# Gated attention in a layered kernel: decay matrix by a low-rank bf16 product, a new order of the work, scores weighed in halves

## The reference

```python
x = concatenate([q, k, v], -1)
ig, fg = x @ Wi + bi, x @ Wf + bf             # one gate of each kind per row and head
log_f_cum = cumsum(log_sigmoid(fg))           # along the sequence
log_D = where(ltr, log_f_cum[s] - log_f_cum[t], -inf) + ig[t]
max_log_D = max(log_D, over t)
D = exp(log_D - max_log_D)
C = (qh @ kh^T / sqrt(16)) * D
normalizer = maximum(abs(sum(C, over t)), exp(-max_log_D))
h = (C / (normalizer + EPS)) @ vh             # then a layer norm inside each head, times ln_scale
```

## Time and profile before

| | us |
|---|---|
| median of 3 runs | 2189.09 (2188.45 to 2192.63) |
| the profiled execution's own time | 2187.51 |
| its span, first to last instruction | 2185.8 |
| `gated_attention` within it | 386.8 |

### The profile page before, as it was taken

One profiled execution on the slowest core, in us unless ns is written; L12 is line 12 of the kernel. 1 busy time (PEld: TensorE's weight loads), 2 busy tenths in 40 slices (PEclk: granted clock), 3 DMA queues, 4 the chain that ended last, 5 costly groups with the idle time before them and its releaser, 6 DMA issues. The chain is left out here.

```text
span 2185.8 us, 34619 instructions
## 1 busy us (share of the span) xinstructions
PE 1499.0 (69%) x11458; PEld 931.5 (43%) x11458; DVE 1441.3 (66%) x2920; ACT 1114.9 (51%) x1540; POOL 570.9 (26%) x910
## 2 busy tenths in 40 slices
PE   3349999999299848788753666548989855776111
PEld 3326555555277635454431233334555542444000
DVE  6648888886245337667764999824555556775796
ACT  4517777777112124333443788822434335777454
POOL 3412333333200032322231444110010001111663
PEclk9999999999599969888985567568999976788555
DMA  5643555553300022113101000011010120000111
GB/s 167 199 109 86 136 129 131 136 131 95 82 1 0 2 66 59 44 38 68 34 6 62 0 1 1 1 37 37 23 37 22 28 82 20 1 1 1 48 49 39
DMA packets 94834, 120.62 MB, mean 55 GB/s; under 512 B 26128, under 2 KB 78552, under 8 KB 90108
## 3 DMA queue, kind: packets, MB, share of 16 engines
q1 hardware_dynamic: 94716, 119.12, 21.2%
HBM read 79.30 MB, written 22.09 MB: 46 GB/s over the span
## 5 line engine op out<-in xcount | busy, mean ns | idle before, releaser
L610 DVE TENSOR_REDUCE ratt_nmax<-ratt_psS 128x2 f32<-128x512 f32 x512 | 318.2, 684 | 92.3 <-PE ratt_psS L502 92.0
L576 ACT ACTIVATE ratt_E<-ratt_psT 128x1024 f32<-128x1024 f32 x256 | 255.0, 1023 | 105.4 <-PE ratt_psT L524 105.4
L502 PE MATMUL ratt_psS<-ratt_K,ratt_Q 72*128 72x256 bf16 x1024 | 204.1, 283 | 38.8 <-DMA ratt_K<-context_parts 33.2
L524 PE MATMUL ratt_psT<-ratt_Q,ratt_K 75*128 75x256 bf16 x1024 | 195.7, 274 | 5.2 <-DMA ratt_Q<-ratt_rows 4.8
L537 PE MATMUL ratt_psO<-ratt_E,ratt_V 128*32 128x256 f32 x2048 | 137.9, 387 | 0.7 <-ACT ratt_E L576 0.7
L502 PEld LDWEIGHTS ratt_psS<-ratt_K,ratt_Q 72*128 72x128 bf16 x1024 | 79.8, 99 | 134.8 <-issue 64.1
L524 PEld LDWEIGHTS ratt_psT<-ratt_Q,ratt_K 75*128 75x128 bf16 x1024 | 99.4, 98 | 22.9 <-DMA ratt_Q<-ratt_rows 5.3
L1355 PE MATMUL gatt_psA<-gatt_DA,gatt_same 128*128 128x512 f32 x128 | 88.4, 780 | 25.3 <-DVE gatt_DB L1240 25.3
L1174 POOL TENSOR_TENSOR gatt_DA<-gatt_own,gatt_a 128x1024 f32<-128x1024 f32 x32 | 61.6, 1937 | 143.1 <-PE gatt_psA L1358 90.0
L3304 PE MATMUL final_psT<-final_identh,final_Z 128*128 128x128 f16 x64 | 8.2, 309 | 110.4 <-ACT final_Z L3338 110.4
L1238 DVE TENSOR_REDUCE gatt_mx<-gatt_psA 128x16 f32<-128x1024 f32 x32 | 39.0, 1220 | 64.0 <-PE gatt_psA L1358 63.4
(11 more groups left out here) (461 smaller groups left out, 4029.4 us busy)
## 6 DMA issues: line engine op xcount, KB each, us to landing
ratt_Q<-z_parts SPq DMA_DIRECT2D x32, 576.0 KB
ratt_K<-context_parts SPq DMA_DIRECT2D x96, 192.0 KB
gatt_V<-in_ctx_dram SPq DMA_DIRECT2D x16, 512.0 KB, 6.2
z_parts<-prep_ZS SPq DMA_DIRECT2D x48, 128.0 KB, 2.7
context_parts<-prep_CS SPq DMA_DIRECT2D x48, 128.0 KB, 2.3
head_sums<-ratt_O SPq DMA_DIRECT2D x64, 72.0 KB
all_X<-in_x_dram SPq DMA_DIRECT2D x8, 512.0 KB
prep_C<-in_ctx_dram SPq DMA_DIRECT2D x8, 512.0 KB
```

The costliest lines, as they stand in the source:

```text
L502: mm = nc.tensor.matmul(psS[:, RING[h], c * D:(c + 1) * D], Q9[0:R, buf, h, k % 2, c * P:(c + 1) * P], K9[0:R, buf, h, k % 2, :], start=Tr ...
L524: mm = nc.tensor.matmul(psT[:, p % 2, e, c, :], K9[0:RM, buf, h, u, c * P:(c + 1) * P], Q9[0:RM, buf, h, u, :], start=True, stop=True)
L576: nc.scalar.activation(E[:, 2 * b + p // 2, 2 * (p % 2):2 * (p % 2) + 2], psT[:, p % 2], ACT.Exp, scale=SCALE).then_inc(exped, 1)
L610: nc.vector.tensor_reduce(nmax[:, k % 2, h, :], psS[:, RING[h]].rearrange("p (c t) -> p c t", c=2), AX.X, ALU.max, negate=True).then_inc(m ...
```

## The change

Only `gated_attention`, two methods of `Heads` and one HBM tensor (`decay_rows`) change. `softmax_attention`, which also uses `Heads`, keeps its form.

- `spread_a`, `max_and_shift`, `DA`, `DB`, `same`, `own`, `mask` and the copy `CG` are gone; the gates read `CT` itself.
- After the running sums PE turns `a` (`turn_a`: 64 rows of 128, one row for each tile and head), VectorE takes the running maximum with two scans (`running_maximum`), PE turns that back (`turn_maximum`), VectorE copies it (`take_maximum`).
- POOL splits `a` and the negated maximum into three bf16 parts each (`split_rows`). SP writes them to HBM, waits, and reads them back in five DMAs into rows of `LT` and `R` (`decay_rows`). The other rows, constant, hold the causal mask against an identity. `decay(t)` is two bf16 products of `LT` and `R` over 94 rows; ScalarE's exponential reads them from PSUM and writes `PB`.
- `weigh` multiplies the scores into `PB` in place, in two halves of eight heads, and the scores and `turn` hand over by half.
- The order is written anew in 46 slots of a quarter group, all unrolled. In slot n PE decays tile n - 6, scores n - 7, turns and multiplies n - 8. Tails run three and four groups behind. `QT` has three buffers.
- ScalarE's slot: (0) softplus; (3) first copy of the turned Z; copies of the turned tile, exponential; (3) second copy of Z; (0) logarithms; (1) a tail's part; output; (2) `place_values(g - 1)`.

Cut to its core:

```diff
+        self.by_half, self.portions = by_half, 2 if by_half else 1
...
-        pe.wait_ge(self.s_taken, g * G + j)
+        pe.wait_ge(self.s_taken, (g * G + j) * self.portions)
...
+            if self.by_half and c == 0:
+                mm.then_inc(self.half_scored, 1)
...
-        pe.wait_ge(self.weighted, t + 1)
+        pe.wait_ge(self.weighted, t * self.portions + 1)
         pe.wait_ge(self.pt_done, t * 2)
         for i in range(NP):
+            if self.by_half and i == NP // 2:
+                pe.wait_ge(self.weighted, t * 2 + 2)
...
+        heads = Heads(nc, s, ident, KX, VB, 3, True)
...
+                def decay_rows(g):
+                    w = g % 2
+                    sp.wait_ge(split, g + 1)
+                    if g > 1:
+                        sp.wait_ge(rows_in[w], (g // 2) * ROWS_IN)
+                    sp.dma_start(rows_dram[w].rearrange("n p h t -> h n p t"), parts[:]).then_inc(rows_out, 16)
+                    sp.wait_ge(rows_out, g * 16 + 16)
+                    if g > 1:
+                        sp.wait_ge(decayed, (g - 1) * G)
+                    for p in range(3):
+                        sp.dma_start(LT[MX_ROW + p * HC:MX_ROW + (p + 1) * HC, w].rearrange(
+                            "h j c u t -> h (j c) (u t)"), rows_dram[w, 1, p].rearrange(
+                                "(x h) t -> h x t", h=HC)).then_inc(rows_in[w], 16)
+                    for u in range(2):
+                        for_u = rows_dram[w, 0].rearrange("p h (u t) -> u p h t", u=2)[u]
+                        sp.dma_start(R[A_ROW + 3 * u:A_ROW + 3 * u + 3, w].rearrange("p j c h t -> p (j c h) t"),
+                                     for_u).then_inc(rows_in[w], 16)
...
+                rows_of_context(0)
+                keys(0, 0)
+                keys(0, 1)
+                for g in range(NG):
+                    decay_rows(g)
+                    if g > 0:
+                        keys(g, 0)
...
+                        sp.wait_ge(v_copied, g * 2 + 2)
+                        rows_of_context(g + 1)
+                    if g > 0:
+                        keys(g, 1)
...
+                    step(gp.tensor_copy(parts[:, :, 0], x))
+                    step(gp.tensor_tensor(rest[:, 0], x, parts[:, :, 0], ALU.subtract))
+                    step(gp.tensor_copy(parts[:, :, 1], rest[:, 0]))
+                    step(gp.tensor_tensor(rest[:, 1], rest[:, 0], parts[:, :, 1], ALU.subtract))
+                    step.end()
+                    gp.tensor_copy(parts[:, :, 2], rest[:, 1]).then_inc(split, 1)
...
+                def running_maximum(g):
+                    step = Steps(dve, pair_steps, PPER, g)
+                    dve.wait_ge(a_turned, g + 1)
+                    if g > 0:
+                        dve.wait_ge(split, g)
+                        dve.wait_ge(m_turned, g)
+                    step(v.tensor_copy(pair[:, 0], psG[0:GH, 0:P]))
+                    for u in range(2):
+                        x = pair[:, 0, u * L:(u + 1) * L]
+                        step(v.tensor_tensor_scan(pair[:, 2, u * L:(u + 1) * L], x, x, LOW, ALU.max, ALU.max))
+                    step(v.tensor_scalar(pair[:, 1], pair[:, 2], -1.0, None, ALU.mult))
...
+                def weigh(t):
+                    dve.wait_ge(d_done, t + 1)
+                    for c in range(KC):
+                        half = heads.PB[:, t % 2, c * HC:(c + 1) * HC, :]
+                        dve.wait_ge(heads.half_scored if c == 0 else heads.scored, t + 1)
+                        v.scalar_tensor_tensor(half, heads.psS[:, c].rearrange("p (h t) -> p h t", t=L),
+                                               float(DH) ** -0.5, half, ALU.mult, ALU.mult).then_inc(heads.weighted, 1)
...
+                for n in range(SLOTS):
+                    g, i = at(n)
+                    if i == 0:
+                        if is_group(g):
+                            front_gates(g)
+                        if is_tile(n - 7):
+                            weigh(n - 7)
+                        if is_group(g - 3):
+                            tail_centre(g - 3)
+                        if is_group(g):
+                            front_logs(g)
...
+                        if is_group(g):
+                            front_sums(g)
+                        if is_group(g - 4):
+                            tail_scale(g - 4)
+                        if is_tile(n - 7):
+                            weigh(n - 7)
+                        if is_group(g + 1):
+                            norm.take_stats(dve, g + 1)
+                        if is_group(g):
+                            running_maximum(g)
+                    if i == 2:
+                        if is_group(g + 1):
+                            if is_group(g):
+                                dve.wait_ge(z_turned, g * KC + KC)
+                            norm.normalise(dve, g + 1, Z)
+                        if is_group(g):
+                            take_maximum(g)
+                        if is_tile(n - 7):
+                            weigh(n - 7)
...
+                def decay(t):
+                    g, j = at(t)
+                    w = g % 2
...
+                    for c in range(KC):
+                        mm = nc.tensor.matmul(psA[:, c, :], LT[0:ROWS, w, j, c].rearrange("p u t -> p (u t)"),
+                                              R[0:ROWS, w, j, c].rearrange("p h t -> p (h t)"), start=True, stop=True)
...
+                for n in range(SLOTS):
+                    g, i = at(n)
+                    t = n - 6
+                    if is_tile(t):
+                        decay(t)
+                    if is_tile(t - 2):
+                        tg, tj = at(t - 2)
+                        heads.turn(pe, tg, tj)
+                    if is_group(g) and i == 2:
+                        turn_maximum(g)
+                    if is_group(g + 1) and i == 3:
+                        turn_z(g + 1, 1)
+                    if is_tile(t - 1):
+                        tg, tj = at(t - 1)
+                        heads.scores(pe, tg, tg % 3, tj)
+                    if is_group(g) and i == 1:
+                        turn_a(g)
+                    if is_group(g + 1) and i == 3:
+                        gates_of(g + 1)
+                    if is_tile(t - 2):
+                        tg, tj = at(t - 2)
+                        if tj == 0:
+                            pe.wait_ge(v_copied, tg * 2 + 2)
+                        heads.values(pe, tg, tg % 2, tj)
+                    if is_group(g) and i == 0:
+                        running_sums(g)
+                    if is_group(g + 1) and i == 2:
+                        turn_z(g + 1, 0)
 
             @block.scalar
             def _(act):
@@ -1393,75 +1453,80 @@
...
+                def exp(t):
+                    act.wait_ge(decayed, t + 1)
+                    if t > 1:
+                        act.wait_ge(heads.turned, 2 * t - 2)
+                    sc.activation(heads.PB[:, t % 2].rearrange("p (c h) t -> p c (h t)", c=KC), psA[:], ACT.Exp).then_inc(
+                        d_done, 1)
...
```

More of the change, by code:

```diff
@@ L1062, in gated_attention @@
         lscale = s.sb("lscale", [P, D])
-        same, tri = s.sb("same", [P, P]), s.sb("tri", [P, P])
-        own = s.sb("own", [P, L])
-        mask = s.sb("mask", [P, HC, L], BF16)
+        tri = s.sb("tri", [P, P])
         one = s.sb("one", [P, 1])
         Z = s.sb("Z", [P, G, D])
-        CG = s.sb("CG", [P, KC, G * P])
         V2 = s.sb("V2", [P, BG, D])
@@ new lines, in keys @@
+                def keys(g, half):
+                    after = g * G - 2 + 2 * half
+                    if after > 0:
+                        sp.wait_ge(heads.scored, after)
+                    for c in range(KC):
+                        for h in range(HC):
+                            rows = slice(h * DH, (h + 1) * DH)
+                            first = g * (G * P) + half * HG
+                            sp.dma_start(KX[rows, half, c, h, :], CT[rows, c, first:first + HG]).then_inc(
+                                heads.kx_in[half], 16)
@@ L1190, in step @@
+                pool.wait_ge(w_in, 144)
+                for g in range(NG + 4):
                     if is_group(g + 1):
@@ new lines, in _ @@
+                query(0, 0)
+                query(0, 1)
+                for n in range(SLOTS):
+                    g, i = at(n)
+                    t = n - 6
+                    if is_group(g) and i == 0:
+                        softplus(g)
+                    if is_group(g + 1) and i == 3:
+                        query(g + 1, 0)
+                    if is_tile(t - 2):
+                        tg, tj = at(t - 2)
+                        heads.copy_turned(act, tg, tj)
+                    if is_tile(t):
+                        exp(t)
+                    if is_group(g + 1) and i == 3:
+                        query(g + 1, 1)
+                    if i == 0:
+                        logarithms(g)
+                    if is_group(g - 3) and i == 1:
```

(5 more changed lines are left out.)

443 lines of the change are left out of this document (186 added, 257 removed).

## The result

The changed kernel takes 2122.38 us (median of 4 runs, 2120.2 to 2125.29), the kernel before 2190.16 beside it: ratio 0.969, 95% interval 0.967 to 0.971. The forecast was 2120. The profiled execution took 2125.29 us, the slowest of the four; its span is 2123.6 at a mean clock of 0.831. The changed stage runs from 766.6 to 1089.9 us, 323.3 us against 386.8. That is 63.5 us less; the stages ahead of it took 5.7 us more in this execution, those behind it 4.3 less (1033.7 against 1038.0), which makes 62.2, the difference of the spans. It comes from one profiled execution of each kernel, and how much it varies between executions was not measured.

A forecast was written before the change was run, and what follows sets the result against it. Bound: a chain through several engines, no engine full. 57.5 + 21.9 + 185.2 + 18.9 + 34.5 = 318 us against 386.8, 69 less; 2187.5 - 69 = 2118.5, with 1.6 above predicted 2120, range 2097 to 2147.

The forecast's parts named there:

- Part 3: Weighing in two halves on VectorE: 0.72 us a half, +0.9 per group, buying between 0 and 0.4 us a slot.
- Part 5: SP's DMA queue: keys 0.70, landing 2.8, reads 3.0; 31.0 us a group, as long as PE; bounds 29.2 and 33.8.
- Part 6: Prologue and end: first decay product at 818.5 us, 14 us lost; 34.5 us from last tile's product to end.
- Part 1: Decay by bf16 products on PE: 0.44 us a tile instead of 2.3; VectorE loses 9.8 us a group, POOL 7.7.
- Part 2: Making the rows adds per group two 0.3 us PE transposes, 1.3 us on VectorE, at most 3 us on POOL.
- Part 4: PE's queue: 25.4 us busy at clock 0.91 plus 5.6 us of waits, a period of 31.0 us.
- the allowance of 4: Later stages only start earlier; their clock alternates between its levels, for which 4 us were allowed.
- rival 3: Slower than before: PE loses its clock; half clock throughout gives 2243 us; decides from a period near 42; chance 0.03.
- Rival 2: Both queues short, PE at full clock and SP at 0.667 per key: period 29.3, stage 305, 2107 us; chance 0.14.

The follow-up runs named there:

- The doubled product: The changed kernel with each decay product issued twice, the second over the first: 2131.50 us, ratio 0.973.
- the logarithms first: The changed kernel with VectorE's difference of the logarithms put ahead of an older group's centring: 2127.59 us, ratio 0.971.
- the filled gap: The changed kernel with ten unread bf16 products in PE's wait before each running sums: 2117.76 us, ratio 0.967.
- the gates filled: The changed kernel with two unread bf16 products after the gates of each of a group's first three tiles: 2118.88 us, ratio 0.967.
- the earlier start: The changed kernel with GpSimd's deviations of group 0 put ahead of this stage's constants: 2126.57 us, ratio 0.970.

## Why the prediction was right, point by point

The time came out inside the range, by the mechanism forecast in the main: PE's queue with VectorE's waits in it sets a period of 31 us. One step failed (the worth of the halves, Part 3), one conclusion was wrong (SP as an equal bound, Part 5), and the closeness of the number is in part luck (Part 6).

- **Part 1** holds: a decay product is 0.60 us for the pair with its latency, 0.44 from start to start; the exponential from PSUM 1.04 (row of 1.02 taken). GpSimd is busy 8.4 us a group, VectorE 23.3.
- **Part 2** holds: the normalisation 2.29 (2 taken, bounds 1.4 and 5.4), the scans 0.30 each, GpSimd's five operations 2.5 us.
- **Part 3**: a half is 0.688 us, between my 0.72 and the 0.66 that the Trainium skill's formula gives (VectorE: DVE Perf Modes, the TRN2 errata). The step that failed is its worth: "between 0 and 0.4 us a slot". Undone, it was 13.4 us over 32 slots, 0.42 a slot, just above the range, and the sum had taken next to nothing for it. The prediction named both places, the reader of a half and a VectorE chain right behind a weighing; the cost in the steady groups lay in the chains (1.05 us a group), and the clock more than doubled it there (2.8).
- **Part 4**: 25.95 us busy at 0.89 plus waits of 3.03, 0.66, 0.25 and 0.99 make 30.9, for 25.4, waits of 3.0, 1.0 and 1.2, and 0.4 for handovers in 31.0. Work and waits were each off by half a microsecond or a little more, in opposite directions. The doubled product shows that this queue is on the path.
- **Part 5** was wrong in what it concluded. In the steady groups the keys are 0.63 to 0.67 us each (0.70 taken), the landing 1.8 (2.8 taken), the reads 2.5 (3.0). SP has 4.1 us left, so its own work is 26.8 us, below the lower bound of 29.2 (whose terms add up to 28.7). The period stood because PE's queue gave the same number. This, not the sum, made the result look better founded than it was.
- **Part 6**: the first decay product came 60.8 us after the stage's start, 57.5 forecast, and not for SP's sake: the rows had been issued by 818.3, the product began at 827.43. PE did the gates of group 1 at half clock ahead of it and then waited 2.9 us for that group's logarithms. From the first to the last decay product it was 224.8 us (226.0 forecast), from there to the end 37.7 (34.5); 4.2 of that was VectorE held up by GpSimd. So the stage took 323.3 us where 318 were forecast: 63.5 us saved, not 69. The stages behind it gave 4.3 back, for which the allowance of 4 stood, and those ahead of it took 5.7 more. By that the profiled execution came out at 2125.3 instead of 2118.5; the median of four is 2.9 below it, where 1.6 above had been taken. That 2122.4 lies so near 2120 is partly luck.
- **Rivals.** The clock, rival 3, was weighed by what one gap does to a whole group. The runs show it at a smaller price: at 0.89 or 0.85 a group's work costs 2.9 or 4.7 us more than the 23.0 of a group at full clock. Shortening a wait (the logarithms first) lowered the clock to between 0.79 and 0.84, filling it raised it. The point where this rival was said to decide, PE's work at 1.8 times its full-clock time, is set too high: 23.1 times 1.8 already makes the period of 42 without any wait; with the 4 us of waits that its own sum has, it is near 1.65. The rule of the Trainium skill cited there (TensorE: Matmul & The Clock Gate, HAM oscillation) speaks of gaps between bursts of matmuls; the filled gap agrees with it, but the second stretch, behind 3.7 us of narrow gates without a gap, is not in that rule. Rival 2 counted for itself that no gap above 3.1 us would be left; behind gaps of 3.03 us the clock fell all the same.

What stays open: why the same work falls to half clock in one group and not in the next. In the run with the halves undone the first of the five groups held full clock with nothing filled, and in the run with the gates filled a wait of 3.03 us had no such stretch behind it. So it is open, too, whether an order exists that holds full clock throughout (28 to 29 us a group, some 14 us over the stage). The run with the gap filled has the lowest median of all, 2117.76 us, below both kernels, but its interval overlaps that of the changed kernel. And no run separates the bf16 decay product from the new order: with the halves undone the two together still save 53 us, and how they share it was not measured.

## What to carry to other kernels

Where TensorE's queue is the bound and has gaps, price a wait twice: by its length, and by the clock that the stretch behind it may lose, read from windows of a few microseconds. Before moving a step on VectorE or GpSimd, look at what the other engine does at the new place; twice here a move that was right by the dependencies was undone by that. Splitting the last operation of a chain is worth what the chains behind it wait. It was worth 13 us in the new order and nothing that the total shows in the old one, where the chain through the maximum was the slower one; that this is the reason was argued, not tested.

## What the runs showed of the hardware that I had not expected

- VectorE and GpSimd can hold each other up for a whole instruction. 128x64 operations of 0.23 and 0.20 us on VectorE took 2.25 and 2.35 beside GpSimd's 128x1024 multiplication and addition, ending within 0.1 us of them, and 0.23 and 0.20 with these gone. The Trainium skill (SBUF — State Buffer, Who interferes with whom) tells of one shared port pair, locked for the whole instruction; the ends of these rows agree. It went the other way too, in the one profile of the earlier start: four selects on GpSimd took 6.51 us instead of 3.07 beside a clearing of 3.47 us on VectorE, and the first of them alone 4.10, ending 0.6 us after it. By the same section a VectorE instruction with at most one SBUF input, outside the two-port modes, does not contend, which would leave a clearing out; this row speaks against it, and the measurement decides.
- The fall of PE's clock behind work without a gap: 0.58 for 3.3 us behind 32- and 34-column matmuls that kept it busy. With wide matmuls among them the group's clock was 0.94 to 1.00 in four groups of five, against 0.89 to 0.94 in the changed kernel. What in that work lets the clock fall was not settled.
